# An attention-weighted gather rebuilt: one spread of stacked taps, blocks of five rows

## The reference, cut to what matters

```python
x = x + attend(_ln_c(x))       # out = sum over 49 taps p of patch_p * attn[:, p]
t = _to_tokens(x)
t = t + _L0_ffn_ref(_ln_t(t), ...)   # routed by mean over an image's tokens, 2 of 8 experts
```

```python
for p in range(K * K):
    ki, kj = divmod(p, K)
    oi, oj = (ki * DIL, kj * DIL)
    patch = xp[:, :, oi:oi + H, oj:oj + W]
    out = out + patch * attn[:, p][:, None, :, :]
```

## Time and profile before

| | us |
|---|---|
| median of 3 runs (lowest, highest) | 1263.26 (1258.61, 1263.72) |
| the profiled execution, its time | 1263.83 |
| its span, first to last instruction | 1261.9 |
| conv_phase, up to | 529 |
| attend_phase, 529 to 783 | 254 |
| ffn_phase, from 783 | 479 |

### The profile page before, as it was taken

One profiled execution on the slowest core, in us unless ns is written; L12 is line 12 of the kernel. 1 busy time (PEld: TensorE's weight loads), 2 busy tenths in 40 slices (PEclk: granted clock), 3 DMA queues, 4 the chain that ended last, 5 costly groups with the idle time before them and its releaser, 6 DMA issues. The chain is left out here.

```text
span 1261.9 us, 19335 instructions
## 1 busy us (share of the span) xinstructions
PE 1128.5 (89%) x7380; PEld 981.5 (78%) x7380; DVE 714.7 (57%) x1719; ACT 494.8 (39%) x923; POOL 236.2 (19%) x160
## 2 busy tenths in 40 slices
PE   4788999999999999578779887699899989989997
PEld 3776666666667665378779887699899989989997
DVE  3554453554454252335754674667677667777676
ACT  4573323323322110132543443645545535445442
POOL 1000000000000000100440462213233222232332
PEclk9788999999999999556775785799999989999999
DMA  9311121022020000233990685423124221421211
GB/s 256 106 38 38 38 75 39 1 86 80 1 65 27 1 12 4 52 85 86 253 270 3 169 244 177 130 71 107 50 76 126 70 70 50 137 75 42 71 51 38
DMA packets 98968, 106.34 MB, mean 84 GB/s; under 512 B 5298, under 2 KB 95699, under 8 KB 98692
## 3 DMA queue, kind: packets, MB, share of 16 engines
q1 hardware_dynamic: 79888, 86.15, 24.0%
q10 hardware_dynamic: 19000, 19.11, 5.0%
HBM read 65.69 MB, written 39.56 MB: 83 GB/s over the span
## 5 line engine op out<-in xcount | busy, mean ns | idle before, releaser
L706 PE MATMUL pM<-V,U 128*128 128x368 f16 (+3 forms) x2016 | 320.9, 316 | 0.0
L706 PEld LDWEIGHTS pM<-V,U 128*128 128x128 f16 x2016 | 197.3, 98 | 108.2 <-issue 1.6
L1473 DVE TENSOR_TENSOR gl<-gf,gh 128x384 fp32r<-128x384 f32 x192 | 161.8, 864 | 63.4 <-ACT gh L1367 63.4
L1367 ACT ACTIVATE gf<-pH,b1c 128x384 f32<-128x384 f32 x192 | 112.1, 584 | 195.3 <-PE pH L1586 146.3
L1601 PE MATMUL pY<-w2h,gh 128*128 128x256 f32 x576 | 168.6, 293 | 17.3 <-DVE z L1485 16.4
L1601 PE MATMUL pY<-w2l,gh 128*128 128x256 f32 x576 | 164.1, 285 | 0.0
L1601 PE MATMUL pY<-w2h,gl 128*128 128x256 f32 x576 | 164.0, 285 | 0.0
L510 DVE TENSOR_TENSOR V<-pV,V 128x384 f16<-128x384 f32 x96 | 53.1, 554 | 164.9 <-ACT V L408 164.9
L1586 PE MATMUL pH<-xh,w1h 128*128 128x384 f32 x384 | 131.7, 343 | 8.5 <-DVE w1l L1444 4.2
L1586 PE MATMUL pH<-xl,w1h 128*128 128x384 f32 x384 | 131.2, 342 | 0.0
L1586 PE MATMUL pH<-xh,w1l 128*128 128x384 f32 x384 | 131.0, 341 | 0.0
(11 more groups left out here) (173 smaller groups left out, 1544.7 us busy)
## 6 DMA issues: line engine op xcount, KB each, us to landing
xa<-in_xt SPq DMA_DIRECT2D x16, 576.0 KB, 4.9
xn_scratch<-xa SPq DMA_DIRECT2D x16, 576.0 KB, 5.9
xn<-xn_scratch SPq DMA_DIRECT2D x16, 576.0 KB, 8.7
xr<-in_xt SPq DMA_DIRECT2D x16, 576.0 KB, 6.8
t_scratch<-ts ACTq DMA_DIRECT2D x16, 576.0 KB, 5.6
tn_scratch<-tn ACTq DMA_DIRECT2D x16, 576.0 KB, 5.2
tnk<-tn_scratch SPq DMA_DIRECT2D x24, 384.0 KB, 3.3
tk<-t_scratch SPq DMA_DIRECT2D x24, 384.0 KB, 3.9
```

Source lines behind the costliest of these rows:

```text
L706: return nc.tensor.matmul(out[:, :, first:end], U[:, hi_u, k, piece, :], V[:, b % 2, hi_v, k, c, :, first + TILES * d:end + TILES * d], st ...
L1367: last = nc.scalar.activation(dst, pH[:, j % 4, 0:CN], ACT.Gelu, bias=b1c[:, j // FB, j % FB:j % FB + 1])
L1473: tt(gl[:, sl, j, :], gf[:, j % 2, :], gh[:, sl, j, :].bitcast(F32), ALU.subtract).then_inc(g_step, 1)
```

## The change

Only `attend_phase` and its tables change; `conv_phase` and `ffn_phase` are the same.
- Tiles become blocks of 5 rows (`BROWS`), 120 pixels (`TB`): 5 per image (`NB`), the last of 4 rows or 96 pixels (`TL`). Every load or store of an image becomes two transfers (`halves`): 4 blocks of 120, and the last of 96 partitions. The unused rows of the last block are set to zero once by DVE.
- The taps' high and low halves are stacked on 98 partitions of `aT`, and `G` is doubled to match, so one matmul gives their sum in PSUM. `aT` holds all 16 images and is loaded at the start in two transfers; `A` holds all matrices, so there is one spread: 44 items of 6 matmuls, 80 moving columns (16 images x 5 blocks), or 64 for row 4 of a block, which the last block hasn't. ACT rounds each item to the high part and DVE subtracts for the low part, one after the other, through 3 banks. x_high and x_low of images 0 and 1 are put between items.
- `A`'s pads need four memsets on POOL for two; only PE's attend waits for them.
- `X` has three buffers (`XB`) for two, so that x_high(n) waits for the attend of image n-3.
- DVE's order is x_low(n+2), sums(n), statistics(n). ACT's is x_high(n+2), store of t(n-1), normalise(n-1), store of tn(n-1).
- All 16 images are accumulated on POOL, in two buffers `acc` for four; PE sums the tokens of a batch item at once, in a bank of its own (`pC`).

```diff
+BROWS = 5
+TB = BROWS * SIDE
+NB = -(-SIDE // BROWS)
+TL = PIX - (NB - 1) * TB
...
-HHS = [(d, h) for d in (-1, 0, 1) for h in range(TR) if (d, h) not in ((-1, TR - 1), (1, 0))]
-GROUPS = 2
-GI = IMGS // GROUPS
-BT = GI * NT
-SLOT = 4
-SBANKS = OBANKS = 4
...
-T_SUMS = 3
...
+HHS = [(d, h) for d in (-1, 0, 1) for h in range(BROWS) if h - R < BROWS * (d + 1) and h + R >= BROWS * d]
+SLOT = 6
+XB = 3
+SBANKS, OBANKS = 3, 4
+SPREAD_SLOTS = SIDE // SLOT
+T_SUMS = (NB + 1) // 2
+T_STEPS = T_SUMS + 2 * NB + 2
+
+
+def window(d, h, w):
+    return TB * d - SIDE * (h - R) - (w - R)
...
-        aT = sb("aT", [TAPS, 2, GI * PIX], F16)
-        A = sb("A", [TT, BLK, 2 * BT, TT], F16)
...
+        aT = sb("aT", [2 * TAPS, N], F16)
+        A = sb("A", [TB, BLK, 2, IMGS, NB, TB], F16)
...
+        X = sb("X", [TB, XB, 2, NB, C], F16)
...
+        pC = ctx.enter_context(nc.psum_tensor("pC", [P, 512], F32))
...
+        def blocks_of(h):
+
+            return NB if (NB - 1) * BROWS + h < SIDE else NB - 1
...
+        def rows_of(t):
+            return TB if t < NB - 1 else TL
...
+        def halves(dram, n, tile):
+
+            at = n * PIX
+            whole = dram[at:at + (NB - 1) * TB, :].rearrange("(t p) c -> p t c", p=TB)
+            return (whole, tile[:, 0:NB - 1, :]), (dram[at + (NB - 1) * TB:at + PIX, :], tile[0:TL, NB - 1, :])
...
-            def load_attn(g):
-                if g > 0:
-                    sp.wait_ge(spread, NU * g)
-                sp.dma_start(aT[:, :, :], attn_d[:, :, g * GI * PIX:(g + 1) * GI * PIX]).then_inc(at_loaded, 16)
...
-            load_attn(0)
+                for src, dst in halves(xt, n, xr[:, n % 2]):
+                    sp.dma_start(dst, src).then_inc(xr_loaded[n % 2], 16)
+
+            for hl in range(2):
+                sp.dma_start(aT[hl * TAPS:(hl + 1) * TAPS, :], attn_d[:, hl, :]).then_inc(at_loaded, 16)
             for load in (load_xn, load_x):
...
-            for n in range(IMGS):
-                if n % GI == 0 and n // GI + 1 < GROUPS:
-                    load_attn(n // GI + 1)
-                if n + 2 < IMGS:
-                    load_xn(n + 2)
-                    load_x(n + 2)
+            for n in range(2, IMGS):
+                load_xn(n)
+                load_x(n)
...
+            for a in range(2):
+                nc.gpsimd.memset(A[:, 0, a, :, :, R * SIDE:TB], 0.0).then_inc(a_zeroed, 1)
+                nc.gpsimd.memset(A[:, 2, a, :, :, 0:(BROWS - R) * SIDE], 0.0).then_inc(a_zeroed, 1)
...
+                if n % BI == 1 and b >= 2:
+                    pool.wait_ge(sums_ready, b - 1)
...
-                if n % BI != 1 and 0 < n <= IMGS - LATE:
+                if n % BI != 1 and n > 0:
                     accumulate(n - 1)
...
-        def spread_out(eng, copy, g, parity, done, between):
-
-            if g == 0:
...
-                    between(0)
-                d, h, k = ITEMS[u]
-                eng.wait_ge(spread, NU * g + u + 1)
-                at = h * SIDE + k * SLOT
-                copy(A[:, d + 1, :, at:at + SLOT],
-                     pS[0:TT, u % SBANKS, 0:SLOT * 2 * BT].rearrange("p (w n) -> p n w", w=SLOT)).then_inc(done, 1)
...
+        def spread_to(hl, u):
+            d, h, k = ITEMS[u]
+            at = h * SIDE + k * SLOT
+            return A[:, d + 1, hl, :, 0:blocks_of(h), at:at + SLOT]
...
+        def spread_from(u):
+            nb = blocks_of(ITEMS[u][1])
+            return pS[0:TB, u % SBANKS, 0:SLOT * IMGS * nb].rearrange("p (w n t) -> p n t w", w=SLOT, t=nb)
...
-                act.wait_ge(xn_loaded[n % 2], 16 * (n // 2 + 1))
-                if n >= 2:
-                    act.wait_ge(o_ready, 3 * (n - 1))
-                nc.scalar.copy(X[:, n % 2, :, 0, :], xn[:, n % 2]).then_inc(xhi_ready, 1)
+                act.wait_ge(xn_loaded[n % 2], 32 * (n // 2 + 1))
+                if n < 2:
+                    act.wait_ge(pads_set, n + 1)
+                if n >= XB:
+                    act.wait_ge(o_ready, T_SUMS * (n - XB + 1))
+                nc.scalar.copy(X[:, n % XB, 0], xn[:, n % 2]).then_inc(xhi_ready, 1)
...
+            def store(n):
+                act.wait_ge(t_step, n * T_STEPS + T_SUMS)
+                for dst, src in halves(t_d, n, ts_[:, n % 2]):
+                    act.dma_start(dst, src).then_inc(t_stored[n % 2], 16)
+
+            def store_tn(n):
+                act.wait_ge(tn_ready, n + 1)
+                for dst, src in halves(tn_d, n, tn[:, n % 2]):
+                    act.dma_start(dst, src).then_inc(tn_stored[n % 2], 16)
...
-                act.dma_start(t_d[rows, :].rearrange("(t p) c -> p t c", p=TT),
-                              ts_[:, n % 2]).then_inc(t_stored[n % 2], 16)
-                act.wait_ge(tn_ready, n + 1)
-                act.dma_start(tn_d[rows, :].rearrange("(t p) c -> p t c", p=TT),
-                              tn[:, n % 2]).then_inc(tn_stored[n % 2], 16)
-
+            for u in range(NU):
+                act.wait_ge(spread, u + 1)
+                nc.scalar.copy(spread_to(0, u), spread_from(u)).then_inc(ahi_spread, 1)
+                if u in (NU // 3, 2 * NU // 3):
+                    x_high(u // (NU // 3) - 1)
...
-                if n % GI == 0:
-
-                    spread_out(act, nc.scalar.copy, n // GI, 0, a_by_act, x_high)
-                    x_high(n + 1)
-                if (n + 1) % GI > 0 and n + 2 < IMGS:
+                if n + 2 < IMGS:
                     x_high(n + 2)
                 if n > 0:
+                    store(n - 1)
                     normalise(n - 1)
-                    store(n - 1)
+                    store_tn(n - 1)
+            store(IMGS - 1)
             normalise(IMGS - 1)
-            store(IMGS - 1)
+            store_tn(IMGS - 1)
...
-                nc.vector.tensor_tensor(X[:, n % 2, :, 1, :], xn[:, n % 2], X[:, n % 2, :, 0, :],
+                nc.vector.tensor_tensor(X[:, n % XB, 1], xn[:, n % 2], X[:, n % XB, 0],
...
+            for u in range(NU):
+                dve.wait_ge(ahi_spread, u + 1)
+                nc.vector.tensor_tensor(spread_to(1, u), spread_from(u), spread_to(0, u), ALU.subtract).then_inc(alo_spread, 1)
+                if u in (NU // 3 + 2, 2 * NU // 3 + 2):
+                    x_low((u - 2) // (NU // 3) - 1)
+            dve.wait_ge(pads_set, 3)
             for n in range(IMGS):
-                if n % GI == 0:
-
-                    spread_out(dve, nc.vector.tensor_copy, n // GI, 1, a_by_dve, x_low)
-                    if n > 0:
-                        statistics(n - 1)
-                    x_low(n + 1)
+                if n + 2 < IMGS:
+                    x_low(n + 2)
                 sums(n)
-                if (n + 1) % GI > 0:
-                    statistics(n)
-                    if n + 2 < IMGS:
-                        x_low(n + 2)
-            statistics(IMGS - 1)
-            dve.wait_ge(sums_ready, 1)
-            total = pS[:, 0, SUM_COLS:SUM_COLS + CC * SUMS].rearrange("p (c e) -> p c e", c=CC)
+                statistics(n)
+            dve.wait_ge(sums_ready, B)
...
-                    after(pe, a_by_dve if u % 2 else a_by_act, (NU * g + u - SBANKS) // 2 + 1)
...
-                        last = nc.tensor.matmul(pS[0:TT, u % SBANKS, o:o + 2 * BT],
-                                                G[:, v, at:at + TT], a[:, :, h * SIDE + w % MO * TILES + w // MO],
-                                                start=True, stop=True)
...
+            def spread_taps(u):
+                d, h, k = ITEMS[u]
+                nb = blocks_of(h)
+                if u >= SBANKS:
+                    pe.wait_ge(alo_spread, u - SBANKS + 1)
+                for w in range(k * SLOT, (k + 1) * SLOT):
+                    at = window(d, h, w) + G0
+                    v = 1 + EDGE.index(w) if w in EDGE else 0
+                    o = (w % SLOT) * IMGS * nb
+                    first = h * SIDE + w % MO * TILES + w // MO
+                    last = nc.tensor.matmul(pS[0:TB, u % SBANKS, o:o + IMGS * nb], G[:, v, at:at + TB],
+                                            aTv[:, :, first:first + (nb - 1) * TB + 1:TB], start=True, stop=True)
+                last.then_inc(spread, 1)
...
+                            ki, ko = rows_of(t + d), rows_of(t)
                             last = nc.tensor.matmul(
-                                pO[0:TT, (3 * n + u) % OBANKS, (t % 2) * C:(t % 2 + 1) * C],
-                                A[:, d + 1, a * BT + (n % GI) * NT + t, :], X[:, n % 2, t + d, x, :],
+                                pO[0:ko, (T_SUMS * n + u) % OBANKS, (t % 2) * C:(t % 2 + 1) * C],
+                                A[0:ki, d + 1, a, n, t, 0:ko], X[0:ki, n % XB, x, t + d, :],
...
+            pe.wait_ge(at_loaded, 32)
+            for u in range(NU):
+                spread_taps(u)
+            pe.wait_ge(a_zeroed, 4)
+            pe.wait_ge(alo_spread, NU)
...
-                if n % GI == 0:
-                    spread_taps(n // GI)
...
-            for e in range(LATE):
```

(56 more changed lines are left out.)

134 lines of the change are left out of this document (55 added, 79 removed).

## The result

The kernel after takes 1274.95 us (median of 4 runs, 1271.84 to 1276.91), the kernel before, on the same chip, 1260.93 us (1256.41 to 1263.72). The ratio is 1.0112, 95% interval 1.0071 to 1.0154: slower by about 14 us. The profiled execution has a span of 1274.4 us, granted clock 0.894.

The account below looks back on a forecast made before the run. PE bounds the spreads, data loads bound attend. Start +6.5, spread +0.9, image 0 -0.4, then 192.1 us against 191.5 to the means: +7.6 on 1263.3 gives 1271, called 1272 for hitches; range 1251 to 1290.

Parts of the forecast that it names:

- load chain: Attend: sums wait for x_low, cast and a load issued only after the previous sums; 1272 us, chance 0.57.
- rival of the uneven split: DMA: 120 rows share worse over sixteen engines; aT load +10.5 us, turn's loads 0.25 us longer; 1279 us, chance 0.15.
- part 1: Start, waiting for the larger aT and G loads: 6.5 us later, range +4.5 to +10.5; pad memsets cost nothing.
- Spread: One spread for two, 44 items of 6 matmuls at 0.137 us or less, plus inserted X work: 41.6 us, range 38 to 46.
- the ring: Spread's three banks, passing from PE to ACT to DVE and back: 2.4 us, 0.80 us an item, just under PE's 0.82.
- Image 0: Start of attend: sums of image 0 end some 7.5 us after the spread, 8.0 before, at 598.1 us.
- The turn: Attend, images 1 to 13: load 8.35, X cast 1.25, x_low 1.49, sums 1.65, hand-overs 0.05; 12.8 us each, 166.4 in all.
- Waits: Attend: ACT's X cast waits for xn 4 to 5 us per image; DVE idles for that cast, no longer the t store.
- Tail: After sums of image 13: last matmuls and sums 11.4 us, then statistics to means 14.3; means at 790.2 us.
- Hidden loads: Attend: xn is there when the cast wants it, 8.75 us an image; 1219 us, chance 0.14.
- Light traffic: Attend: the pair of loads lands in 6.8 us or less, turn 11.2 us; 1251 us, chance 0.06.
- Slow spread: Spread: 98 rows or the two-step ring run at half pace, 66 us for 41.6; 1296 us, chance 0.08.

Follow-up runs that it names:

- e1: Kernel after with x_low(n+2) put back behind sums and statistics of image n on DVE: 1219.18 us, ratio 0.9673 to the kernel before.
- e2: Kernel after, DVE's order kept, with SP issuing the load of xn(n+1) ahead of x(n): 1203.74 us, ratio 0.9566 to the kernel before.
- e3: Kernel before with a third X buffer and x_low(n+2) ahead of the sums of image n on DVE: 1320.43 us, ratio 1.0468.
- e6: Kernel after with xn(n+1) issued ahead of x(n) on SP, and each aT half loaded as 48 rows and 1: 1201.98 us, ratio 0.9527.
- e7: Kernel after with the spread's matmuls reading neighbouring elements of aT instead of ones 240 B apart; output not the layer's; one run: 1269.96 us.
- e8: Kernel before with SP issuing xn of image n+3 ahead of x of image n+2: 1244.63 us, ratio 0.9890 to the kernel before.
- e9: Kernel after with tn of each image stored a second time, to an unread scratch: 1309.17 us, ratio 1.0387 to the kernel before.
- e5: Kernel after with both order edits, SP issuing xn(n+1) before x(n) and DVE's x_low(n+2) behind sums and statistics: 1198.63 us, ratio 0.9531.
- e4: Kernel before with every image load and store of attend cut in two transfers, five tiles and one: 1260.27 us, ratio 0.9997.

## Why the prediction was right

It gave 1272 us, slower, by the load chain, with a range of 1251 to 1290; 1274.95 was measured, and the chain is shown by the waits, by e1, which breaks it in one place, e2, which breaks it in another, and e3, which makes it in the other kernel. By its steps:

- **Start.** +6.5 us forecast; the spread starts at 547.07 in place of 542.5, +4.6, the lower end of its range. The memsets of the pads on POOL (13.07 us) lie in that wait, as written. The rival of the uneven split asked for +10.5, and that term falls; e6 shows why (fewer packets at once, each faster). Its other term, 0.25 us more a turn for loads of 120 rows, is just what the turn came out longer by, and no run changes the rows of those loads, so it stays open. Of the prediction's two sums for it, 1279 follows from its range for part 1 (+4 over 6.5); the 1278 beside it counts +3 there.
- **Spread.** 41.6 us forecast up to attend's first matmul, 43.8 measured (547.07 to 590.90), made of two wrong sizes that nearly cancel. The term 36 x 0.83 + 8 x 0.69, 35.4 us, was too low: PE is busy 41.69 us. I had scaled 0.164 us by columns, from 96 to 80, to 0.137; it is 0.160, 2.0 ns a column where it was 1.7, and the elements that it reads now stand 240 B apart where they stood 192 B apart. e7 shows that the spaced read is what costs: 0.100 us with neighbours. The inserted X work and the last copies, 4.6 + 1.6 us, were too high: 43.8 - 41.7 = 2.1 us. They follow from each other: with 0.16 us a matmul PE needs 0.96 us an item, the ring 2.5 us for three, 0.83 an item, and there was slack to take the casts in.
- **Image 0.** Sums end at 597.34, forecast 598.1. That this is so near is luck too: the start came out 1.9 us shorter and the spread 2.2 us longer.
- **The turn.** 12.8 us forecast, 13.05 measured: the load 8.65 for 8.35, the engines 4.40 for 4.44. Thirteen turns took 167.96 us for 166.4. PE, statistics, normalising and stores lie beside the load, as forecast. That the load came so close is luck. I took it from pairs of loads in the kernel before, where at 600.01 us the first packet came after 1.0 us and the packets took 6.6; in a gated turn it is 3.1 and 5.1. So less traffic shortened the packets by more than the 0.65 us that I took off the median, and a term that I hadn't, 2 us more before the first packet, made up for it. SP spends 2.4 of those 3.1 us issuing x; one transfer of the kernel before took 0.31. In e3, with one transfer for each load, the first packet still comes only after 2.1 to 2.2 us. What holds it back stays open.
- **Waits.** The profile shows the named ones, in every image, but ACT's is 9.6 us (124.9 / 13) and not 4 to 5: ACT is free sooner than I had counted. DMA share 0.64 for 0.65. Waits for the t store fell from 21.3 us to 2.4.
- **Tail.** 25.7 us forecast, 27.3 measured: the sums of image 15 end at 777.58, 12.3 for 11.4, and the last token sum has the means at 792.62, 15.0 for 14.3.

```profile
787.99 4.43 PE L1130 MATMUL pC<-ones,acc 120*128 120x1 f32 x20 [10.87 <-POOL acc L959]
...
792.45 0.17 DVE L1086 TENSOR_SCALAR mean<-pC 128x8 f32<-128x8 f32 x1 [12.36 <-PE pC L1130]
```

- **The sum.** Slower by 8.7 us was forecast (1272 for 1263.3), 14.0 was measured by the two medians, the kernel before having come out at 1260.93 this time. By the profiles, the means come at 792.6 for 790.2, 10.0 us later than before. The other 2.5 us of the profiled difference (12.5) lie in the FFN, whose code is unchanged: from its first load to the end it took 478.8 us in the profile of before and 481.3 in that of after, and 476.6 to 482.0 over all profiles of this study. So it is scatter by all that the runs show, not the change.
- **The other rivals.** Hidden loads, 1219: did not come by itself, and "the order of SP, which I can't get round" was the right place; with it changed the time is 1204. Light traffic, a load of 6.8 us or less: 8.65 measured. Slow spread, 66 us: 43.8.

## What to carry to other kernels

Before an operation is moved ahead of another on an in-order engine, follow what it waits for back to a transfer, and that transfer to what gates its issue: here a subtraction put ahead of the sums waited for a load queued behind a load that waited for the sums, and 55 us hung on one call. Break such a loop where it costs least; the queue that issues the loads is the place to look first, and here it also took out waits that had been in the kernel all along (14 us by the ratio in e8). A DMA share of 0.6 can be full stretches and half-empty ones in turn, so cut the windows by the parts of a turn before anything is called free; and a load's time from issue to use has a part before its first packet, which the added bytes of e9 left as it was; it has to be a term of its own.

## What the runs showed of the hardware that I had not expected

- Attend moves 296 to 315 GB/s with a share of 0.96 to 0.99 when nothing gates it (e2, e5), 300 at 1.00 in e8. In a gated turn of the kernel after it is 164 GB/s in the 3.1 us before the first packet of x or xn and 243 GB/s in the 5.2 us of their packets, with a peak of 343 GB/s for one microsecond (640.1 to 641.1 us). Much of the gap to 300 is thus the start and the end of the burst.
- A higher DMA share went with a lower rate: 0.93 and 181 GB/s against 0.68 and 203 (e6 and e2). The share counts the time that packets take, not what they bring.
- Matmuls with 80 moving columns started every 0.160 us when the columns were read 240 B apart and every 0.100 us when they were neighbours, both at the granted clock 0.50, which is 1.2 GHz. With 96 columns 192 B apart it was 0.164. So at the wider spacing a column cost 2.0 ns for 1.7, and sixteen columns fewer saved 0.004 us. As neighbours, 64 columns took the same 0.100 us as 80.
- Two x transfers (120 x 4 tiles, then 96 rows) hold SP's queue for 2.4 us in the gated turn, for 0.85 us in most turns of e1, and for 0.85 to 2.0 us in e2, where the DMA share is 0.96. So it isn't the mean traffic that makes it long; what does stays open. Doubling the transfers in the kernel before cost nothing (e4).
